# Second half's x: cast to two half-precision tiles in SBUF and transposed by DMA instead of by TensorE

## The reference, cut to what matters

```
xn = layernorm(x, gamma, beta)                   # over the 512 channels
up = einsum('lbd,ed->lbe', xn, W_in) + b_in      # e = 1536
uc = short causal convolution of up over l, 3 taps, per channel
x0, x1, v = split(uc, 3)
v  = v * x1
y  = longconv(v, k) + v * conv_bias              # over l, per channel
y  = (y * x0) @ W_out.T
x  = layernorm(x + y)
...                                              # attention-like sublayer, then a quantised FFN
```

## Time and profile before

| | |
|---|---|
| median of three runs | 1066.54 us |
| the profiled execution | 1063.69 us, its span 1061.9 us |
| PE busy | 1006.2 us (95%), 4679 matmul records |
| DVE, ACT, POOL busy | 799.3, 599.9, 552.7 us |
| DMA | 144.65 MB, mean 136 GB/s |
| granted TensorE clock | 0.989 on average |

### The profile page before, as it was taken

How to read it: one execution, slowest core, us unless ns; L and a number is a source line. 1 busy time by engine, 2 the same in 40 slices (tenths; PEclk the granted TensorE clock), 3 DMA queues, 4 the chain that set the end, 5 groups by cost and what they waited for, 6 DMA issues and landing times.

```text
span 1061.9 us, 14827 instructions
## 1 busy us (share of the span) xinstructions
PE 1006.2 (95%) x4679; PEld 602.9 (57%) x4679; DVE 799.3 (75%) x1509; ACT 599.9 (56%) x728; POOL 552.7 (52%) x886
## 2 busy tenths in 40 slices
PE   3899999999999999978999999999999999999985
PEld 2455545544445555456666666666666666666641
DVE  7967975786475567657888888888888888888862
ACT  5655544112566558114666666767576767676664
POOL 5320310221000004269787887878787878787861
PEclk9999999999999999989999999999999999999998
DMA  9323655456475777441444544444444444444334
GB/s 322 61 60 120 203 152 163 145 165 194 162 227 189 241 259 255 141 143 51 105 98 113 105 113 108 115 106 117 104 117 105 109 114 101 122 99 114 76 64 91
DMA packets 178220, 144.65 MB, mean 136 GB/s; under 512 B 99988, under 2 KB 132792, under 8 KB 176120
## 3 DMA queue, kind: packets, MB, share of 16 engines
q1 hardware_dynamic: 178168, 144.00, 49.3%
HBM read 89.29 MB, written 33.70 MB: 116 GB/s over the span
## 4 chain that ended last, share of the span: by engine, by line
PE 50%; DVE 2%; POOL 1%; ACT 1%; DMA 1%; issue 1%; POOLq 0%; DVEq 0%; ACTq 0%
PE conv_bank L1398 28%; PE hq_bank L1421 9%; PE ff_bank L1442 5%; PE back_bank L1442 5%; PE back_bank L1412 1%; PE back_bank L1381 1%; PE ctx_bank L1369 1%; DMA hq_t<-hq_int 0%; POOL sum L1742 0%; DVE z L1607 0%; DVE g_max L1674 0%; POOL sum L1744 0%; ACT g L1546 0%; DMA xq_t<-xq_int 0%; ACT hq_f L1507 0%
## 5 line engine op out<-in xcount | busy, mean ns | idle before, releaser
L1742 POOL TENSOR_TENSOR sum<-z 128x640 f32<-128x640 f32 x128 | 198.2, 1549 | 11.6 <-DVE z L1619 9.6
L837 DVE SCALAR_TENSOR_TENSOR conv_all<-u,taps,conv_all 128x1024 f32<-128x1024 f32 x92 | 122.4, 1331 | 93.2 <-ACT conv_all L708 91.4
L1398 PE MATMUL conv_bank<-block_diag 128*128 128x288 f32 x628 | 167.8, 411 | 1.8 <-DVE z L1619 1.8
L1398 PE MATMUL conv_bank<-kv,block_diag 128*128 128x288 f32 x640 | 168.6, 406 | 0.9 <-DVE z L1619 0.8
L1398 PEld LDWEIGHTS conv_bank<-kv,block_diag 128*128 128x128 f32 x640 | 117.8, 190 | 31.6 <-DVE z L1619 1.8
L1398 PEld LDWEIGHTS conv_bank<-block_diag 128*128 128x128 f32 x628 | 117.3, 193 | 32.4 <-DVE z L1619 2.2
L1421 PE MATMUL hq_bank<-x_lo,hq_t 128*128 128x512 f16 x512 | 122.2, 382 | 4.7 <-DMA hq_t<-hq_int 4.7
L1674 DVE TENSOR_REDUCE g_max<-g 128x1 f32<-128x512 f32 x128 | 85.8, 673 | 41.5 <-ACT g L1546 41.5
L700 ACT ACTIVATE u<-slot_bank,bias,unscale 128x1024 f32<-128x1024 f32 x46 | 55.4, 1204 | 108.9 <-PE slot_bank L509 88.6
L1744 POOL TENSOR_TENSOR sum<-sum 128x320 f32<-128x320 f32 x128 | 111.3, 869 | 10.0
L1607 DVE TENSOR_TENSOR z<-conv_bank,qx 128x512 f32<-128x512 f32 x128 | 88.0, 687 | 34.2 <-PE conv_bank L1398 24.6
(11 more groups left out here) (181 smaller groups left out, 1676.2 us busy)
## 6 DMA issues: line engine op xcount, KB each, us to landing
x_quad<-in_w SPq DMA_DIRECT2D x10, 1024.0 KB, 8.3
v_scratch<-conv_all SPq DMA_DIRECT2D x16, 512.0 KB, 3.5
c_scratch<-v_tok SPq DMA_DIRECT2D x8, 1024.0 KB, 5.3
y<-c_scratch SPq DMA_DIRECT2D x8, 1024.0 KB, 4.9
res<-in_x SPq DMA_DIRECT2D x32, 256.0 KB, 2.9
x_scratch<-res SPq DMA_DIRECT2D x32, 256.0 KB, 3.1
block_diag<-in_ctx SPq DMA_DIRECT2D x32, 256.0 KB, 3.7
block_diag<-ssm_scratch SPq DMA_DIRECT2D x32, 256.0 KB, 3.7
```

The lines of the kernel that those rows point to most:

```text
L837: ins = nc.vector.scalar_tensor_tensor(out=acc, in0=(u_first[kind] if n < 3 else u)[:, t0 + tap:t0 + tap + T // 2, :].rearrange("p t b -> ...
L1398: last = nc.tensor.matmul(view(conv_bank[tb % 2][:, hh, :], 0, (ROW64, T // 2), (1, PAIRS)), toep[:, head.buf, (tb - sb_) * P:(tb - sb_ + ...
L1742: nc.gpsimd.tensor_tensor(sum2[:, :, :], z[:, b, :, 0:half], z[:, b, :, half:2 * half], ALU.add).then_inc(sum2_done, 1)
```

## The change

TensorE no longer turns the second half's quads. Instead, ScalarE casts the normalised quad in SBUF to float16 (`make_hi`), VectorE subtracts that from the quad into a second float16 tile (`make_lo`), and ScalarE issues a transposing transfer for each of the two (`turn_halves`), 16 blocks each, into the quad's part of `x_hi` or `x_lo`. The float16 tiles lie in buffers that are free at that point: `conv[X1]`, `conv[V]`, `v_tok` and `conv[X0]` for the quads 0 to 3. `x_hi` and `x_lo` are laid out quad by quad. The places in the order: the casts of quads 0 and 1 behind ScalarE's slots 20 and 23; the subtraction of quad 0 behind VectorE's slot 22 and those of quads 1, 2 and 3 behind tokens 2, 9 and 12. The first transfer waits for TensorE's last slot of the first half. SyncE's loads into the quad buffers wait for `lo_made` instead of `x_turned`.

```diff
-        QUAD_AT = {1: 0, 4: 1, 9: 2, 13: 3}
+        HI_AT = {20: 0, 23: 1}
+        LO_AT = {22: 0}
+        LATE_LO_AT = {2: 1, 9: 2, 12: 3}
...
+        half_rows = [view(tile, 0, (1, T * P)).bitcast(F16) for tile in (conv[X1], conv[V], v_tok[:, :], conv[X0])]
+        def token_half(q, low):
+            return view(half_rows[q], low * QUAD * D, (1, QUAD * D))
+        def by_chunk(ap, step_dc, step_t):
+            return view(ap, 0, (step_dc, DC), (step_t, QUAD), (1, P))
...
                     if Q >= NQ + 2:
-                        sp.wait_ge(x_turned, DC * (Q - 1))
+                        sp.wait_ge(lo_made, Q - NQ - 1)
...
                     if i < 2:
-                        sp.wait_ge(x_turned, DC * (HALF * NQ - 1 + i))
+                        sp.wait_ge(lo_made, NQ - 1 + i)
...
-                        elif hf > 0 and s < 2 and j < 2:
-                            pe.wait_ge(made, DC * (NQ * hf + 2 * (s + 1)))
+                        elif hf > 0 and s < 2 and j == 0:
+                            for q in group:
+                                pe.wait_ge(halves_turned[2 * pr + q], 2 * 16)
...
-                        if hf + 1 < HALF and t in QUAD_AT:
-                            turn_quad(NQ * (hf + 1) + QUAD_AT[t])
...
+                def make_hi(q):
+                    act.wait_ge(x_normed, q + 1)
+                    if q == 0:
+                        act.wait_ge(vx_done, 2 * DC)
+                    elif q == 1:
+                        act.wait_ge(v_stored, 2 * 16 * DC)
+                    elif q == 2:
+                        act.wait_ge(c_stored, 16 * DC)
+                    else:
+                        act.wait_ge(y_done, 4 * DC)
+                    src = quad_buf(NQ + q)[:, :, :].rearrange("p t d -> p (t d)")
+                    nc.scalar.copy(by_chunk(token_half(q, 0), QUAD * P, P), by_chunk(src, P, D)).then_inc(hi_made, 1)
+
+                def turn_halves(q):
+                    if q == 0:
+                        act.wait_ge(slot_full, NSLOT)
+                    for low, (made, x) in enumerate(((hi_made, x_hi), (lo_made, x_lo))):
+                        act.wait_ge(made, q + 1)
+                        act.dma_start_transpose(view(x[:, q, :, :], 0, (P, DC * QUAD), (1, P)), token_half(q, low)).then_inc(halves_turned[q], 16)
...
                     if hf + 1 < HALF:
-                        for q in range(NQ):
-                            split_hi(NQ * (hf + 1) + q)
+                        turn_halves(0)
+                        turn_halves(1)
+                        make_hi(2)
+                        turn_halves(2)
+                        make_hi(3)
+                        turn_halves(3)
...
+                def make_lo(q):
+                    dve.wait_ge(hi_made, q + 1)
+                    src = quad_buf(NQ + q)[:, :, :].rearrange("p t d -> p (t d)")
+                    hi, lo = (by_chunk(token_half(q, low), QUAD * P, P) for low in range(2))
+                    nc.vector.tensor_tensor(lo, by_chunk(src, P, D), hi, ALU.subtract).then_inc(lo_made, 1)
...
+                        if more and s in LO_AT:
+                            make_lo(LO_AT[s])
...
-                        if more and t in QUAD_AT:
-                            split_lo(nxt + QUAD_AT[t])
+                        if more and t in LATE_LO_AT:
+                            make_lo(LATE_LO_AT[t])
```

More of the change, by code:

```diff
@@ L88, in hyena_block @@
         shift = sb("shift", [P, NQ, QUAD])
-        x_hi, x_lo = w["x_hi"], w["x_lo"]
+        x_hi, x_lo = (view(w[name][:, :, :], 0, (DC * QUAD * P, NQ), (QUAD * P, DC), (1, QUAD * P)) for name in ("x_hi", "x_lo"))
         u = sb("u", [P, T + TAPS - 1, P])
@@ L144, in hyena_block @@
         x_lo_done = sem("x_lo_done")
+        hi_made = sem("hi_made")
+        lo_made = sem("lo_made")
+        halves_turned = [sem(f"halves_turned{q}") for q in range(NQ)]
         u_zeroed = sem("u_zeroed")
@@ L457, in _ @@
             def _(pe):
-                def free_bank(Q, dc):
-                    hf, q = divmod(Q, NQ)
-                    if q == 0:
-                        pe.wait_ge(ch_copied, 4 * hf * DC - 3 + dc)
-                    else:
-                        pe.wait_ge(x_lo_done, DC * (Q - 1) + dc + 1)
                 def turn_quad(Q):
@@ L468, in turn_quad @@
                         n = DC * Q + dc
-                        if dc == 0 and Q < NQ:
+                        if dc == 0:
                             pe.wait_ge(x_normed_first, Q + 1)
-                        elif dc == 0:
-                            pe.wait_ge(x_normed, Q - NQ + 1)
-                        if Q >= NQ:
-                            free_bank(Q, dc)
-                        elif n >= 4:
+                        if n >= 4:
                             pe.wait_ge(x_lo_done, n - 3)
@@ L507, in slot @@
                             for q in group:
-                                cols = slice((2 * pr + q) * 512, (2 * pr + q + 1) * 512)
-                                last = nc.tensor.matmul(slot_bank[n % 2][:, q, :], wt[:, dc, e * P:(e + 1) * P], xt[:, dc, cols],
+                                last = nc.tensor.matmul(slot_bank[n % 2][:, q, :], wt[:, dc, e * P:(e + 1) * P], xt[:, 2 * pr + q, dc, :],
                                                         start=(j == 0 and dc == 0), stop=(j == 2 and dc == DC - 1))
@@ L512, in slot, with convolve @@
                         last.then_inc(slot_full, 1)
-                def convolve(hf, cc, others=(), quad=None):
+                def convolve(hf, cc, others=()):
                     first = chain_counts(hf, cc)
@@ L521, in convolve @@
                     for k in range(4):
-                        if quad is not None:
-                            pe.wait_ge(x_lo_done, DC * quad + k + 1)
-                        elif not others:
+                        if not others:
                             pe.wait_ge(ch_copied, first - 4 + k + 1)
@@ L639, in _ @@
                         for cc in pieces_after(s):
-                            others, quad = (), None
+                            others = ()
                             if hf == 0 and cc < DC - 1:
                                 others = [(w_lo_done, KINDS * (cc + 2))] + [(wout_done, DC)] * (cc == 0)
-                            elif hf > 0 and cc == 0:
-                                quad = NQ * (hf + 1) - 1
                             if hf == 0 and cc == 0:
@@ L650, in _ @@
                                 pe.wait_ge(mean_made, 1)
-                            convolve(hf, cc, others, quad)
+                            convolve(hf, cc, others)
                     for t in range(PARTIAL):
@@ L679, in split_hi @@
                         act.wait_ge(x_turned, n + 1)
-                        nc.scalar.copy(x_hi[:, dc, q * 512:(q + 1) * 512], x_bank(n)[:, :, :].rearrange("p t b -> p (t b)")).then_inc(x_hi_done, 1)
+                        nc.scalar.copy(x_hi[:, q, dc, :], x_bank(n)[:, :, :].rearrange("p t b -> p (t b)")).then_inc(x_hi_done, 1)
+                def make_hi(q):
[16 more added lines that the diff above has]
+                        act.dma_start_transpose(view(x[:, q, :, :], 0, (P, DC * QUAD), (1, P)), token_half(q, low)).then_inc(halves_turned[q], 16)
                 def slot(hf, s):
@@ L784, in _ @@
                             copy_conv(hf, cc)
+                        if hf == 0 and s in HI_AT:
+                            make_hi(HI_AT[s])
                         if hf + 1 == HALF and s in SQUARE_AT:
@@ L823, in split_lo @@
                         dve.wait_ge(x_hi_done, n + 1)
-                        cols = slice(q * 512, (q + 1) * 512)
-                        nc.vector.tensor_tensor(x_lo[:, dc, cols], x_bank(n)[:, :, :].rearrange("p t b -> p (t b)"), x_hi[:, dc, cols], ALU.subtract).then_inc(x_lo_done, 1)
+                        nc.vector.tensor_tensor(x_lo[:, q, dc, :], x_bank(n)[:, :, :].rearrange("p t b -> p (t b)"), x_hi[:, q, dc, :], ALU.subtract).then_inc(x_lo_done, 1)
+                def make_lo(q):
[3 more added lines that the diff above has]
+                    nc.vector.tensor_tensor(lo, by_chunk(src, P, D), hi, ALU.subtract).then_inc(lo_made, 1)
                 def slot(hf, s):
```

## The result

The changed kernel took 1074.2 us (median of 12 runs, 1068.1 to 1079.3), the kernel before 1065.7 us on the same chip (12 runs, 1061.7 to 1068.8). The ratio is 1.0081 (95% interval 1.0061 to 1.0101): slower, by 8.5 us, where 3.6 were forecast. Both are the same kernel, and their intervals overlap. A single execution strays by up to 4 us from its median before and by up to 6 us after. The profiled execution of the changed kernel is the longest of its twelve, 1079.25 us with a span of 1077.5, so its stamps are later than those of a typical run.

A forecast was written before the change was run, and what follows sets the result against it. Landing times on SP's queue, then one square on ACT, were taken to bound the first half's end, not PE. Terms -0.65 + 2.55 + 1.7 = +3.6 us on 1066.54 gave about 1070.1 us, range 1065.6 to 1074.0.

The forecast's parts named there:

- What bounds the kernel: First half's end: landing times on SP's queue, then one square on ACT, set the fifth slot; PE not in that chain.
- PE and DVE: Up to the fifth slot: 8.5 us less PE work, some 1.7 showing at the first slot, none at the fifth.
- The -0.65 us in SP's chain: DVE term: earlier issue around quad 2's load gains 0.45 us, shorter subtractions 0.2; ends -1.2 and 0.
- The transfers' own size: Each 16-block transposing transfer takes 2.5 us of all engines and 4.35 us to landing.
- their place at the start: The first three transfers go at about 187, behind y's load, and are free, with 3 us of cover.
- The collisions of the late five: Transfers beside SP's chain: 0.3 us plus three at 0.75, +2.55 us; low half of quad 2 costs nothing.
- the upper end of +5: Collision term's worst case: every transfer's 2.5 us of engines paid in the two tail cycles.
- The clock: Behind the fifth slot: after some 5.7 us idle PE drops to half clock, +1.7 us, ends 0 and +3.7.
- Sum: Whole kernel: -0.65 + 2.55 + 1.7 = +3.6 us, about 1070.1 us, slower by 0.34%; chance 0.50.
- (a): Rival, no change: collisions find room and clock costs 1.7 or nothing, -0.65 to +2.1, about 1067.3 us; chance 0.30.
- (c): Rival at the second slot: quad 3's low half lands after 253.6; at landing 258, 6.1 us, 1072.6; chance 0.07.
- (b): Rival at first and fifth slots: PE's saving arrives, w1's load issued before about 252.6, -3.8 us, 1062.7; chance 0.08.

The follow-up runs named there:

- e3: The changed kernel without its eight transposing transfers, TensorE waiting for casts and subtractions instead: 1063.69 us, ratio 1.0007 against the kernel before.
- e4: The kernel before with only 16 of the second half's 64 transposes, all else unchanged: 1064.44 us, ratio 1.0017 against the kernel before.
- e1: The changed kernel with its first transposing transfer held until y's last quarter has loaded: 1069.58 us, ratio 1.0066 against the kernel before.
- a2: The changed kernel itself, unaltered, measured again beside the experiments: 1071.08 us, ratio 1.0064 against the kernel before.
- e12: The changed kernel with only the first three transposing transfers, the other five left out: 1065.46 us, ratio 1.0012 against the kernel before.
- e7: e1 with w1's first two loads issued by ACT behind its last transfer instead of by SP: 1067.61 us, ratio 1.0037 against the kernel before.
- e9: e1 with SP's store of token t put ahead of the residual load of token t+3, both halves: 1059.29 us, ratio 0.9963 against the kernel before.
- e5: The changed kernel with the same eight transposing transfers issued from SP's queue instead of ACT's: 1069.46 us, ratio 1.0049 against the kernel before.
- e10: The kernel before with only SP's order turned, store of token t ahead of residual load of token t+3: 1061.90 us, ratio 0.9982.
- e6: The changed kernel with each transposing transfer issued in two pieces of 8 blocks on ACT's queue: 1069.56 us, ratio 1.0042 against the kernel before.

## Why the prediction was wrong

*What bounds the kernel: right.* PE is not in the chain (e3, e4). SP's issue of w1's load and the square behind it set the fifth slot, in the changed kernel too.

*PE and DVE.* No gain from 8.5 us less of PE's work at the fifth slot: right (e3: +0.7). The subtraction took 2.28 us for 2.3 forecast and the cast 1.90 for about 2. The -0.65 us in SP's chain did not show: the way is 64.2 in e3, not below 62.7, though such a difference is smaller than two executions differ by. The first slot was to start at 244.5: e1 has 244.36, e3 245.47, a2 248.44 and the long profiled execution 256.13.

*The transfers' own size: right on the engines, short to landing; their place at the start: wrong.* They were to take 2.5 us of the engines, and took about 2.6. 16 blocks were to land in 4.35 us; in e1, high halves took 4.4 us at best, 4.6 in the median, low halves 5.4 to 6.2. The first three, however, were said to go at about 187, behind y's load, and to be free. They go from 184.82, ahead of it, because ACT's queue runs ahead of its activations, and they stretch y's load from 4.8 to 9.9 (a2) and 12.9 us. The step was wrong, and e12 prices it at some 0.6 us.

*The collisions of the late five: this is the step that failed.* The forecast had 0.3 + 3 x 0.75 = 2.55 us, with the price of one read off output stores that ran beside 8-block transfers (3.4 in place of 2.9 us). Measured, the late five cost about 6 us: e1 against e3 is +5.9 by medians, and in the profiles their ways differ by 5.1 us. That is just above the upper end of +5 that the prediction gave, in which every transfer's 2.5 us of engines in the tail cycles are paid. What was wrong is the price of a meeting and one place that was held for free. The us from issue to landing of SP's stores in the stretch, by token, with the transfer that is in flight beside each:

| store of token | before | e3 | e1 | a2 | after | transfer beside it |
|---|---|---|---|---|---|---|
| 7 | 3.5 | 4.0 | 4.2 | 4.0 | 4.1 | high half of quad 2 |
| 8 | 3.1 | 3.1 | 5.3 | 5.1 | 5.7 | low half of quad 2 |
| 9 | 2.2 | 3.0 | 3.2 | 3.2 | 3.3 | |
| 10 | 2.0 | 2.6 | 4.5 | 4.5 | 4.0 | high half of quad 3 |
| 11 | 3.0 | 3.1 | 4.4 | 6.0 | 4.6 | low half of quad 3 |
| 12 | 3.0 | 3.2 | 3.4 | 3.3 | 3.2 | |
| 13 | 3.4 | 5.1 | 5.3 | 3.2 | 5.2 | |
| 14 | 3.0 | 3.0 | 3.1 | 3.3 | 3.3 | |

The three transfers and SP's stores 8, 10 and 11 in e1; the residual load behind each store goes 0.02 us after the store has landed, so it marks the landing:

```profile
229.03 1.98 ACTq L698 DMA_TRANSPOSE x_lo<-v_tok  x1
...
237.40 3.12 ACTq L698 DMA_TRANSPOSE x_hi<-conv_all  x1
243.03 1.76 ACTq L698 DMA_TRANSPOSE x_lo<-conv_all  x1
```

```profile
230.33 0.70 SPq L302 DMA_DIRECT2D x_scratch<-res  x1
235.65 0.33 SPq L297 DMA_DIRECT2D res<-in_x  x1
...
239.65 0.93 SPq L302 DMA_DIRECT2D x_scratch<-res  x1
244.16 0.33 SPq L297 DMA_DIRECT2D res<-in_x  x1
244.53 1.15 SPq L302 DMA_DIRECT2D x_scratch<-res  x1
248.95 0.33 SPq L297 DMA_DIRECT2D res<-in_x  x1
```

The store of token 7 goes at 225.70 in e1 and that of token 15 at 262.29, 36.6 us for eight links of the chain. The same two stores are 30.7 us apart in e3 (228.83 to 259.50), 28.8 in e12 (230.60 to 259.42) and 28.4 before (227.51 to 255.93). e1 has lost nothing up to token 7, where it is the earliest of the four (the store of token 2 lands 1.3 us later than in e3, beside the low half of quad 1 that was priced at 0.3, but none of that is left), and 5.9 us more than e3 behind it. Three links carry 5.3 of the 5.9: the one behind token 8 is 2.1 us longer than in e3, that behind token 10 is 1.9 and that behind token 11 is 1.3; the other five together are 0.6 longer. The prediction had three meetings at 0.75 us, at most 1.0, taken from 8-block transfers. Three is what there are, but they cost 1.3 to 2.1 us each in e1 and up to 2.9 in a2. And they are not the same three: the high half of quad 2 cost next to nothing (0.3), and the low half of quad 2, held for free because SP waited for DVE there, was the dearest in e1. That wait was some 0.8 and 1.2 us at tokens 9 and 10 before; in e3 only 0.1 and 0.5 us of it are left, and in e1 none. Each longer landing is paid in full, since the next load and store are held until it.

*The clock: it fell where and by what was forecast; that it reaches the end isn't shown.* After an idle of 2.14 us and of 2.96 (e4), eight matmuls take 1.90 us. After 5.92 us (e1) they take 3.59:

```profile
274.53 3.59 PE L511 MATMUL slot_bank<-x_hi,w_hi 128*128 128x512 f16 x8 [5.92 <-ACT conv_all L726]
```

That is the forecast's 1.7 us. In the changed kernel the idle was 4.06 us, and the windows on either side of it say the same (granted clock third from the right):

```profile
280.30:284.30 4.00, 0.01 (x1) 0.00 (x0) 0.00 (x0) 4.00 (x5) 0.00 (x0) 0.95 0.48 185
284.40:288.00 3.60, 3.60 (x11) 1.32 (x12) 3.53 (x3) 3.60 (x3) 0.00 (x0) 0.60 0.00 0
288.00:292.00 4.00, 4.00 (x20) 1.83 (x19) 3.92 (x4) 1.20 (x3) 0.00 (x0) 1.00 0.46 135
```

The clock was granted at 0.60 on average over 3.6 us (1.2 GHz for most of it), then 1.00. In a2 the idle at this slot is only 0.72 us and the clock holds; there it had dropped at the first and second slot, in time that PE would have idled anyway. The length of one idle doesn't decide it: behind 3.78 us (e7, first slot) eight matmuls took 1.89 us, behind 2.41 us (e9, second slot) 3.43.

*Sum.* e1 by its profile: the fifth slot at 274.53 for 269.19 is +5.3, the clock +1.7, together +7.0, and its ratio says +7.0. That the two agree is in part luck: e1's whole span is only 4.3 us longer than before (1066.2 and 1061.9), for of 7.2 us at the first convolution of the second half (297.09 and 289.92) only 5.3 are left where the head stage begins (465.27 and 459.93). e3 shows the same: +4.6, then +2.3, and a ratio of +0.7. So in these profiles a part of what moves the fifth slot doesn't reach the end, where the prediction held that all of it would. The forecast had +1.9 and +1.7.

*The rivals.* (a), no change, and (c), transfers too late for the second slot, were both wrong. The latter came only in e5, where SP's place for the last transfer was late. (b), that PE's saving arrives, was priced at -3.8 us and given little, as SP's order stood against it. That was the right reason: with the order turned and no transfers the saving arrives (-8.0), and with the transfers -3.9 are left.

*Left open.* Where the us between the fifth slot and the head stage go, and what e10 gains in which half. Why the high half of quad 2 cost nothing. Why turned bytes hold up their neighbours more than plain ones, beyond their longer time on the engines, isn't settled; nor whether the 8.5 and 6.8 us of the two measurements differ by more than chance. What part of e6's possible gain is from shorter pieces wasn't separated from noise.

## What to carry to other kernels

Before work is taken off the busiest engine, find what the next stage waits for. Here three quarters of the saving on an engine at 95% was worth nothing, because a ring of stores and loads on one queue set the end; putting a ready store ahead of a load that must wait, in both halves, was worth 1.9 us by itself, and it let 6 to 7 us of PE's saving through when no transfer ran. Traffic added beside a chain whose pace is landing times is paid in full at each store that it meets: take the price of a meeting from the whole time that the new transfer needs of the engines (here 2.6 us, and 1.3 to 2.9 us were paid), not from what a smaller one did to its neighbour, and count no place as free because of a wait that the change itself uses up. And a transfer on a computing engine's queue needs its own wait if it is to start after something, since the queue doesn't keep to that engine's activations.

## What the runs showed of the hardware

- A transposing transfer of 0.5 MB and a 1 MB load in flight together slow each other: the load took 9.9 to 12.9 us for 4.8, the transfer up to 14.5 us for 4.4, and the issue instruction of the next one stood for 12.02 us.
- Five transposing transfers took about 2.6 us each of all 16 engines, plain copies of the same bytes 1.4 (from the DMA shares of one window).
- Beside such a transfer a 256 KB store landed in 4.0 to 6.0 us for 2.6 to 3.1 in e3 (tokens 8, 10 and 11), but in 4.0 to 4.2 for 4.0 beside the high half of quad 2.
- ACT's queue issued a transfer at 184.82 us while an activation of 185.78 and a cast of 186.87, ahead of it in the program, hadn't begun.
- The granted clock held behind an idle of 3.78 us (e7) and fell behind one of 2.41 us (e9).
